# A plain first cycle for the first expert of a Strassen-like stage, and an earlier place for the rounding of raw weight blocks

## The chip, the cores and the metric

The kernel runs on one core of a Trainium2 chip. The metric is the device time of one execution in microseconds (us). In the text and the rows, PE is TensorE, PEld its weight loads, ACT is ScalarE, DVE is VectorE, POOL is GpSimd and SP is SyncE.

## The reference

The reference is a chain: a dense mixture of eight experts and a shared one (the stage "cond", which the change touches), an attention with distances, a second dense-and-typed feed-forward, and a transformer block with routed experts. The stage in question computes, for x of 32 x 64 tokens by 256:

```python
g = jnp.einsum('bsd,edf->ebsf', h, Wg)
u = jnp.einsum('bsd,edf->ebsf', h, Wu)
expert_outs = jnp.einsum('ebsf,efd->ebsd', jax.nn.silu(g) * u, Wd)
expert_output = jnp.einsum('be,ebsd->bsd', gating_probs, expert_outs)
shared = jnp.einsum('bsf,fd->bsd', jax.nn.silu(h @ Sg) * (h @ Su), Sd)
return (1.0 - sg) * expert_output + sg * shared
```

with D = 256 and F = 1024, everything in float32.

## The kernel before, in words

The stage is `paired_experts` (from L222). It holds E = 9 experts (eight and the shared one). A product in float32 is made of three matmuls of rounded parts: high by high, high by low, low by high (`product`, L310). The high part is a rounding copy on ScalarE, the low part a subtraction on POOL (weights) or VectorE (x and the hidden values).

Per expert there are CY = 8 cycles: J = 4 blocks j of the hidden dimension (a pair of 128 rows each) by 2 halves p of the tokens (1024 tokens each, a left and a right side of 512). A cycle does two `quad`s, u = 0 for the gate matrix and u = 1 for the up matrix. Each quad is a 2 x 2 by 2 x 2 block product with seven products in Winograd's form (P1 to P7) instead of eight: it needs the sums S1 to S4 of weight blocks and T1 to T4 of x blocks, and additions of results on the way. The additions: `keep` on ScalarE copies P1 and P5 out of PSUM, `combine` (L544, L547) and `lower_right` (L554) on VectorE add. Between the products of a quad TensorE does the down projections of the cycle before (`down`, four groups of six matmuls in a cycle), so a full cycle is 42 + 24 = 66 matmuls of 512 columns.

Behind the products: ScalarE takes the silu of the four quarters of the gate result (L452), VectorE multiplies by the four of the up result (`hidden`, L561), ScalarE rounds (`round_hidden`), VectorE splits off the low part (`split`, L566), and TensorE uses both in the next cycle's `down`.

The weights of the next expert are prepared meanwhile. `raws(e, j)` rounds the three raw blocks that are used as they are (two ScalarE copies), and POOL splits them (L662, L663) and then makes the four sums in place in the loaded buffer (L665 to L670). `sums(e, j)` rounds the sums (one ScalarE copy) and the block of the down matrix, POOL splits both (L680, L686). The order is written out by hand in `tasks`, which both engines call at the end of their part of cycle c: c = 5, 6, 7 do `raws` 0, 1, 2 of the next expert, c = 6, 7 also `sums` 0, 1 ahead of it; c = 0 does `sums` 2 and `raws` 3 of the own expert, c = 1 `sums` 3. SyncE loads the next expert's weights when the last split of the own ones is done.

The first expert is different. x comes as four tiles of 512 tokens. TensorE turns (transposes) tiles 0 and 1 into the four y_ps banks, ScalarE and VectorE copy them out (`keep_raw`), and from these copies T1 to T4 are made (VectorE), rounded (ScalarE, `round_x`) and split (VectorE, `split_x`). Tiles 2 and 3 are turned between the products of cycle 0. POOL makes the second half's T values (`t_right`, L696 to L701) after a DMA has copied the first half of x to memory (`spilled[0]`, tensor x_saved), since they are written over it; the raw block 2 and its sums lie behind them in POOL's order. Ahead of that copy SyncE issues the loads of x, of the constants and of small tensors (L3138).

Of the kernel before, what the change touches and what calls it, by code (L numbers as in the profile page):

```python
# [6 lines left out]
F32 = mybir.dt.float32  # L7
# [195 lines left out]
def paired_experts(nc, m, x, saved, stage, experts, hyp):  # L203
# [20 lines left out]
    dn_rounded, dn_ready = sem("dn_rounded"), sem("dn_ready")  # L224
    p1_done, p2_done, p3_done, p4_done, p5_done, p6_done, p7_done = (sem(f"p{i}_done") for i in range(1, 8))
# [11 lines left out]
    with ExitStack() as s:  # L237
# [7 lines left out]
        h_hi, h_lo = sb("h_hi", [P, 4, TW], F32R), sb("h_lo", [P, 4, TW], F32R)  # L245
# [8 lines left out]
        t_room = [h, flat[:, 0:4 * TW].rearrange("p (i n) -> p i n", i=4)]  # L254
# [24 lines left out]
        with nc.Block() as block:  # L279
# [29 lines left out]
            def _(pe):  # L309
                def product(bank, e, c, u, w, i, opens, done):  # L310

                    p, j = divmod(c, J)
                    for k, (ws, xs) in enumerate(((w_hi, x_hi(i, 1, cols(p))), (w_hi, x_lo[:, i:i + 1, cols(p)]), (w_lo, x_hi(i, 1, cols(p))))):
                        ins = pe.matmul(bank, ws[:, j, u, w], xs.rearrange("p o n -> p (o n)"), start=(opens and k == 0), stop=(k == 2), skip_group_check=True)  # L314
                    ins.then_inc(done, 1)
# [23 lines left out]
                def quad(e, c, u, between):  # L339
                    p, j = divmod(c, J)  # L340
                    q, g = 2 * (CY * e + c) + u, CY * e + c
                    start = isinstance(g, int) and g == 0
                    if p == 0 and u == 0:
                        pe.wait_ge(up_ready, J * e + j + 1)
                    if start and u == 0:
                        pe.wait_ge(x_lo_dve, 2)
                    if isinstance(g, int) and g == J and u == 0:
                        pe.wait_ge(x_lo_pool, 7)
                    if u == 1:
                        pe.wait_ge(silu_done, 4 * g + 1)  # L350
                    elif not start:
                        pe.wait_ge(h_made, 4 * (g - 1) + 1)
                    product(bank_a, e, c, u, A11, B11, True, p1_done)
                    if u == 1:
                        pe.wait_ge(silu_done, 4 * g + 2)
                    elif not start:
                        pe.wait_ge(h_made, 4 * (g - 1) + 2)
                    product(bank_d, e, c, u, S1, T1, True, p5_done)
                    if start and u == 0:
                        pe.wait_ge(x_lo_dve, 3)  # L360
                    if not start:
                        pe.wait_ge(h_made if u == 1 else silu_done, 4 * g)
                    product(bank_b[u], e, c, u, S2, T2, True, p6_done)
                    pe.wait_ge(p1_kept, q + 1)
                    product(bank_a, e, c, u, A12, B21, False, p2_done)
                    between(0)
                    if start and u == 0:
                        pe.wait_ge(x_lo_dve, 6)
                    pe.wait_ge(u4_made, q + 1)
                    product(bank_d, e, c, u, S4, B22, False, p3_done)  # L370
                    product(bank_b[u], e, c, u, S3, T3, False, p7_done)
# [4 lines left out]
                def turn_right(n):  # L376
                    if n == 0:
                        pe.wait_ge(raw_by_act, 2)
                        pe.wait_ge(raw_by_dve, 2)
                    pe.wait_ge(x_loaded[2 + n], 16)  # L380
                    for k in range(KC):
                        turn(2 + n, k)

                def expert(e, first, last):
                    for c in range(CY):
                        for u in range(UPS):
                            if first and c == 0:
                                quad(e, c, u, turn_right if u == 0 else lambda n: None)
                                continue
# [7 lines left out]
                for t in range(2):  # L397
                    pe.wait_ge(x_loaded[t], 16)
                    for k in range(KC):
                        turn(t, k)  # L400
# [6 lines left out]
            def _(act):  # L407
# [28 lines left out]
                def keep(e, c, u):  # L436
# [3 lines left out]
                    if not (isinstance(q, int) and q == 0):  # L440
                        act.wait_ge(u2_made, q)
                    copy(p1_row[:], bank_a).then_inc(p1_kept, 1)
                    act.wait_ge(p5_done, q + 1)
                    if u == 1:
                        act.wait_ge(silu_done, 4 * g + 3)
                    elif not (isinstance(g, int) and g == 0):
                        act.wait_ge(h_made, 4 * (g - 1) + 3)
# [22 lines left out]

                def expert(e, first, last):
                    for c in range(CY):
                        g = CY * e + c
                        keep(e, c, 0)
                        if not (first and c == 0):
                            pe_e, pe_c = (e, c - 1) if c > 0 else (e - 1, CY - 1)
                            round_hidden(pe_e, pe_c, 11, 3)
                            round_hidden(pe_e, pe_c, 21, 4)
                            act.wait_ge(h_ready, 4 * g)
                        silu(e, c, p2_done, bank_a, 0)  # L480
                        silu(e, c, p3_done, bank_d, 1)
                        silu(e, c, c22_made, p5_row[:], 2)
                        silu(e, c, p4_done, bank_b[0], 3)
                        keep(e, c, 1)
                        if first and c == 0:
                            act.wait_ge(turned, 2 * TT)
                            for t in range(2):
                                keep_raw(1, t)
# [16 lines left out]
                        tasks(e, c, first, last, sums, raws)  # L505
# [4 lines left out]

                stage.load_up_first(act, experts(0)[0:2])
# [3 lines left out]
                for t in range(2):  # L515
                    keep_raw(0, t)
                act.wait_ge(t_made, 1)
                round_x(0, T1, 1)
                act.wait_ge(raw_by_dve, 1)
                round_x(0, B11, 2)  # L520
                act.wait_ge(t_made, 2)
                round_x(0, T2, 1)
                act.wait_ge(w_summed, 4)
                copy(w_hi[:, 0, :, S2:S1 + 1].rearrange("p u (k s) n -> p u k (s n)", k=KC), raw_up[:, :, :, pair(0)]).then_inc(sums_rounded, 1)
                round_x(0, B22, 1)
                act.wait_ge(t_made, 4)
                round_x(0, T3, 1)
                round_x(0, T4, 1)
                raws(0, 1)
# [5 lines left out]
            def _(dve):  # L535
# [3 lines left out]
                def combine(e, c, u):  # L539

                    q = 2 * (CY * e + c) + u
                    dve.wait_ge(p1_kept, q + 1)
                    dve.wait_ge(p6_done, q + 1)
                    dve.tensor_tensor(bank_b[u], p1_row[:], bank_b[u], ALU.add).then_inc(u2_made, 1)  # L544
                    dve.wait_ge(p5_kept, q + 1)
                    dve.wait_ge(u2_made, q + 1)
                    dve.tensor_tensor(bank_d, p5_row[:], bank_b[u], ALU.add).then_inc(u4_made, 1)  # L547

                def lower_right(e, c, u):
# [3 lines left out]
                    dve.wait_ge(u4_made, q + 1)  # L553
# [43 lines left out]
                def split_x(i, n, count):  # L597
                    dve.wait_ge(x_rounded, count)
                    src = raw[0][:, 0:2, sides[0]] if i == B11 else raw[0][:, 1:2, sides[1]] if i == B22 else t_room[0][:, i - T1:i - T1 + n]
                    dve.tensor_tensor(x_lo[:, i:i + n, cols(0)], src, x_hi(i, n, cols(0)), ALU.subtract).then_inc(x_lo_dve, 1)  # L600

                def expert(e, first, last):
                    for c in range(CY):
                        p, j = divmod(c, J)
                        combine(e, c, 0)
                        if not (first and c == 0):
                            pe_e, pe_c = (e, c - 1) if c > 0 else (e - 1, CY - 1)
# [2642 lines left out]
```

## Time and profile before

| | |
|---|---|
| median of 3 runs | 2121.78 us (2121.76 to 2122.68) |
| the profiled execution's own time | 2122.61 us |
| its span | 2120.8 us |
| busy shares: PE, DVE, ACT, POOL | 91%, 70%, 53%, 42% |
| mean granted TensorE clock | 0.959 |

A busy time is the sum of the instructions of an engine. A row of the timeline has its start from the span's start, its duration, the engine, line, operation, tiles written and read, and in brackets the idle time before it and what ended it. The expert stage lasts from the start to about 1105 us; the part around the first expert to about 110 us.

### The profile page before, as it was taken

The page shows a single profiled execution, that of the slowest core. Times are in us where ns is not written, and L with a number is a line of the kernel's source. Part 1 is how long each engine was busy: PE and PEld are TensorE (multiplying, and loading weights), DVE is VectorE, ACT ScalarE, POOL GpSimd, SP SyncE. Part 2 cuts the span into 40 slices and gives each one's busy share as a digit, 9 for nine tenths or more (in the row PEclk, how much of TensorE's full clock was granted, in tenths as well). Part 3 has the DMA queues.
Part 4 walks back from the last instruction along what each step waited for, and adds up shares of the span by engine and source line. Part 5 has one row for each costly group of instructions (what it writes and reads, how often), then busy time and mean ns, then how long its engine had stood idle before and what let it go on. Part 6 is the DMA issues. An engine that isn't in the chain of part 4 may idle for free. (4 is left out here: it accounts for less than half of the span.)

```text
span 2120.8 us, 35303 instructions
## 1 busy us (share of the span) xinstructions
PE 1928.9 (91%) x12206; PEld 1612.7 (76%) x12206; DVE 1476.1 (70%) x2400; ACT 1115.2 (53%) x2117; POOL 897.8 (42%) x858
## 2 busy tenths in 40 slices
PE   5999999999999999999998677999899766959998
PEld 4778878787887878788787466788799645849998
DVE  6777777767777776777876896433588575856776
ACT  4555554545555464555554697232355364636664
POOL 5442241504224150422400185220388234968885
PEclk9999999999999999999999788999999887979999
DMA  4101010010101001010102201310256114556661
GB/s 151 60 1 60 1 59 0 0 59 0 59 0 59 0 0 59 0 59 0 28 1 60 61 3 41 120 45 5 70 195 200 53 29 131 184 183 208 210 214 54
DMA packets 96322, 144.51 MB, mean 68 GB/s; under 512 B 15358, under 2 KB 72608, under 8 KB 96096
## 3 DMA queue, kind: packets, MB, share of 16 engines
q1 hardware_dynamic: 89168, 127.21, 18.6%
q0 software_dynamic: 4928, 12.86, 1.7%
q10 hardware_dynamic: 2128, 3.15, 0.4%
q8 instruction: 60, 0.98, 0.2%
q14 instruction: 38, 0.31, 0.0%
HBM read 111.46 MB, written 14.16 MB: 59 GB/s over the span
## 5 line engine op out<-in xcount | busy, mean ns | idle before, releaser
L314 PE MATMUL ps<-cond_x_lo,cond_w_hi 128*128 128x512 f32 x1008 | 393.7, 391 | 0.0
L408 ACT ACTIVATE cond_h_hi<-cond_h 128x512 fp32r<-128x512 f32 x288 | 177.1, 629 | 266.5 <-DVE cond_h L561 266.4
L566 DVE TENSOR_TENSOR cond_h_lo<-cond_h,cond_h_hi 128x512 fp32r<-128x512 f32 x288 | 261.8, 938 | 4.1 <-ACT cond_h_hi L408 0.3
L314 PE MATMUL ps<-cond_x_hi_first,cond_w_hi 128*128 128x512 f32 x576 | 229.5, 398 | 17.7 <-DVE ps L547 8.8
L662 POOL TENSOR_TENSOR cond_w_lo<-cond_stage_up,cond_w_hi 128x512 fp32r<-128x512 f32 x36 | 57.5, 1596 | 439.0 <-ACT cond_w_hi L408 439.0
L330 PE MATMUL ps<-cond_h_hi,cond_d_hi 128*128 128x512 f32 x576 | 227.4, 395 | 7.3 <-DVE cond_h_lo L566 7.1
L314 PE MATMUL ps<-cond_x_hi_first,cond_w_lo 128*128 128x512 f32 x576 | 225.1, 391 | 0.0
L330 PE MATMUL ps<-cond_h_hi,cond_d_lo 128*128 128x512 f32 x576 | 224.7, 390 | 0.0
L330 PE MATMUL ps<-cond_h_lo,cond_d_hi 128*128 128x512 f32 x576 | 224.3, 389 | 0.0
L452 ACT ACTIVATE cond_h<-ps 128x512 f32<-128x512 f32 x216 | 121.5, 597 | 193.3 <-DVE cond_h_lo L566 151.9
L544 DVE TENSOR_TENSOR ps<-cond_p_row,ps 128x512 f32<-128x512 f32 x144 | 99.8, 693 | 175.7 <-PE ps L314 175.7
L314 PEld LDWEIGHTS ps<-cond_x_lo,cond_w_hi 128*128 128x128 f32 x1008 | 189.9, 188 | 38.0
L408 ACT ACTIVATE cond_p_row<-ps 128x512 f32<-128x512 f32 x288 | 172.1, 598 | 46.5 <-PE ps L314 34.1
L680 POOL TENSOR_TENSOR cond_w_lo<-cond_stage_up,cond_w_hi 128x1024 fp32r<-128x1024 f32 x36 | 86.8, 2410 | 224.9 <-ACT cond_w_hi L408 224.9
L561 DVE TENSOR_TENSOR cond_h<-cond_h,ps 128x512 f32<-128x512 f32 x216 | 147.4, 683 | 45.9 <-PE ps L314 45.9
L314 PE MATMUL ps<-cond_x_hi,cond_w_hi 128*128 128x512 f32 x432 | 169.0, 391 | 1.0 <-DVE cond_p_row L554 1.0
L314 PE MATMUL ps<-cond_x_hi,cond_w_lo 128*128 128x512 f32 x432 | 168.5, 390 | 0.0
L314 PEld LDWEIGHTS ps<-cond_x_hi_first,cond_w_hi 128*128 128x128 f32 x576 | 108.3, 188 | 55.5 <-DVE ps L547 24.4
L330 PEld LDWEIGHTS ps<-cond_h_hi,cond_d_hi 128*128 128x128 f32 x576 | 108.1, 188 | 40.3 <-issue 9.4
L314 PEld LDWEIGHTS ps<-cond_x_hi_first,cond_w_lo 128*128 128x128 f32 x576 | 108.6, 188 | 22.9
L330 PEld LDWEIGHTS ps<-cond_h_hi,cond_d_lo 128*128 128x128 f32 x576 | 108.1, 188 | 23.0
L1031 DVE SCALAR_TENSOR_TENSOR dense_h_lo<-ps,dense_h_hi 128x512 fp32r<-128x512 f32 x64 | 44.3, 692 | 116.4 <-ACT dense_h_hi L977 116.3
(408 smaller groups left out, 5190.2 us busy)
## 6 DMA issues: line engine op xcount, KB each, us to landing
moe_stage_up<-in_L_ffn_expert_wv SPq DMA_DIRECT2D x22, 1024.0 KB, 9.3
typed_stage_up<-in_L_cond_wi SPq DMA_DIRECT2D x11, 1024.0 KB, 4.9
typed_stage_dn<-in_L_cond_wo SPq DMA_DIRECT2D x11, 1024.0 KB, 5.6
moe_stage_dn<-in_L_ffn_expert_proj SPq DMA_DIRECT2D x11, 1024.0 KB, 5.6
cond_stage_up<-in_L_cond_Wg SPq DMA_DIRECT2D x7, 1024.0 KB, 5.1
cond_stage_up<-in_L_cond_Wu SPq DMA_DIRECT2D x7, 1024.0 KB, 7.2
cond_stage_dn<-in_L_cond_Wd SPq DMA_DIRECT2D x7, 1024.0 KB, 9.5
rope_v_now<-rope_v_blk SPq DMA_DIRECT2D x16, 272.0 KB, 2.4
```

The lines of the kernel that those rows point to most:

```text
L314: ins = pe.matmul(bank, ws[:, j, u, w], xs.rearrange("p o n -> p (o n)"), start=(opens and k == 0), stop=(k == 2), skip_group_check=True)
L330: ins = pe.matmul(y_ps[side][d], w[:, 2 * j + r, d * P:(d + 1) * P], xs[:, tile], start=(j == 0 and r == 0 and k == 0), stop=(j == J - 1 a ...
L408: copy = lambda dst, src: act.activation(dst, src, ACT.Copy)
L452: act.activation(h[:, tile], src, ACT.Silu).then_inc(silu_done, 1)
L544: dve.tensor_tensor(bank_b[u], p1_row[:], bank_b[u], ALU.add).then_inc(u2_made, 1)
L561: dve.tensor_tensor(h[:, tile], h[:, tile], src, ALU.mult).then_inc(h_made, 1)
L566: dve.tensor_tensor(h_lo[:, tile], h[:, tile], h_hi[:, tile], ALU.subtract).then_inc(h_ready, 1)
L662: pool.tensor_tensor(w_lo[:, j, :, A11:A12 + 1], raw_up[:, :, :, upper(j)], w_hi[:, j, :, A11:A12 + 1], ALU.subtract)
L680: pool.tensor_tensor(w_lo[:, j, :, S2:S1 + 1].rearrange("p u (k s) n -> p u k (s n)", k=KC), raw_up[:, :, :, pair(j)], w_hi[:, j, :, S2:S1 ...
L1031: dve.scalar_tensor_tensor(h_lo[:, st % HB], up_ps[st % 2][0], 0.0, h_hi[:, st % HB], ALU.max, ALU.subtract).then_inc(h_ready, 1)
```

## The change

Two things are changed.

Cycle 0 of the first expert no longer uses the seven products. `plain` multiplies the blocks as they are: eight products for each matrix, accumulated in pairs in PSUM, so that no `keep` and no `combine` is needed; VectorE copies one of the four results out of PSUM (`plain_copy`) so that the following steps find it where it was. One more block (the lower left one) is needed raw; it lies in the room of S1 of block 3. x is rounded straight from PSUM (`raw_block`) and split straight from PSUM (`split_block`), with the fourth x block in the room of T4 of the other half; the copies `keep_raw` come later. T1 to T4 are made and split during cycle 0, for cycle 1, in a tile of their own. The transposes of tiles 1 to 3 stand between the plain products. `raws(0, 1)` on ScalarE now stands between the roundings of the first and the second x tile, and on POOL ahead of the split of sums 0. Since cycle 0 keeps nothing, the counts of five semaphores start lower by two.

In all other cycles, of all experts, `tasks` is split in two: `raw_tasks` stands behind the first silu of the cycle on ScalarE and ahead of the sums on POOL, `sum_tasks` stays at the end.

```diff
-        def tasks(e, c, first, last, sums, raws):
-            nxt = e + 1
+        def raw_tasks(e, c, first, last, raws):
             if c == 0 and not first:
-                sums(e, 2)
                 raws(e, 3)
-            elif c == 1 and not first:
-                sums(e, 3)
             elif c >= 5 and not last:
-                if c > 5:
-                    sums(nxt, c - 6)
-                raws(nxt, c - 5)
+                raws(e + 1, c - 5)
+        def sum_tasks(e, c, first, last, sums):
+            if c < 2 and not first:
+                sums(e, c + 2)
+            elif c > 5 and not last:
+                sums(e + 1, c - 6)
...
 # TensorE
+                def plain():
+                    for u in range(UPS):
+                        plain_left(u)
+                        turn_tile(1 if u == 0 else 3)
+                        plain_lower_left(u)
+                        plain_right(u)
+                        if u == 0:
+                            turn_tile(2)
+                        plain_lower_right(u)
+                def plain_left(u):
+                    if u == 0:
+                        pe.wait_ge(plain_ready, 1)
+                        pe.wait_ge(x_lo_dve, 1)
+                    else:
+                        pe.wait_ge(silu_done, 1)
+                    multiply(bank_a, 0, u, A11, B11, cols(0), True).then_inc(p1_done, 1)
+                    if u == 0:
+                        pe.wait_ge(x_lo_dve, 2)
+                    multiply(bank_a, 0, u, A12, B21, cols(0), False).then_inc(p2_done, 1)
...
 # ScalarE
+                def plain():
+                    silu(0, 0, p2_done, bank_a, 0)
+                    act.wait_ge(t_made, 1)
+                    round_x(0, T1, 1)
+                    silu(0, 0, p3_done, bank_d, 1)
+                    act.wait_ge(t_made, 2)
+                    round_x(0, T2, 1)
+                    silu(0, 0, c22_made, p5_row[:], 2)
+                    silu(0, 0, p4_done, bank_b[0], 3)
+                    act.wait_ge(t_made, 4)
+                    round_x(0, T3, 1)
+                    round_x(0, T4, 1)
+                    act.wait_ge(turned, 2 * TT)
+                    for t in range(2):
+                        keep_raw(1, t)
...
+                def first_group(e, c, first, last):
+                    g = CY * e + c
+                    keep(e, c, 0)
...
+                    act.wait_ge(h_ready, 4 * g)
+                    silu(e, c, p2_done, bank_a, 0)
+                    raw_tasks(e, c, first, last, raws)
+                    silu(e, c, p3_done, bank_d, 1)
+                    silu(e, c, c22_made, p5_row[:], 2)
+                    silu(e, c, p4_done, bank_b[0], 3)
...
                 raws(0, 0)
-                act.wait_ge(turned, 2 * KC)
...
+                copy(w_hi[:, J - 1, :, S1], raw_up[:, :, 0, lower(0)]).then_inc(plain_rounded, 1)
+                for k in range(KC):
+                    act.wait_ge(turned, k + 1)
+                    raw_block(k, 0)
+                raws(0, 1)
+                for k in range(KC):
+                    act.wait_ge(turned, KC + k + 1)
+                    raw_block(k, 1)
...
 # POOL
-                raws(0, 0)
+                pool.wait_ge(w_rounded, 1)
+                split_upper(0).then_inc(plain_ready, 1)
+                split_lower(0).then_inc(plain_ready, 1)
+                pool.wait_ge(plain_rounded, 1)
+                pool.tensor_tensor(w_lo[:, J - 1, :, S1], raw_up[:, :, 0, lower(0)], w_hi[:, J - 1, :, S1], ALU.subtract).then_inc(plain_ready, 1)
+                pool.wait_ge(plain_ready, 3)
+                sum_blocks(0, 0)
+                raws(0, 1)
                 split_sums(0, 0)
-                raws(0, 1)
                 split_sums(0, 1)
```

## Rows read from the trace of the kernel before

**Rows 1.** The page, busy time, share of the span, instructions.

```profile
PE 1928.9 (91%) x12206; PEld 1612.7 (76%) x12206; DVE 1476.1 (70%) x2400; ACT 1115.2 (53%) x2117; POOL 897.8 (42%) x858
```

**Rows 2.** Timeline of TensorE, first products and starts of cycles 2, 4, 5.

```profile
21.80 0.79 PE L314 MATMUL ps<-cond_x_hi_first,cond_w_hi 128*128 128x512 f32 x1 [7.86 <-POOL cond_w_lo L680]
22.39 0.63 PE L314 MATMUL ps<-cond_x_lo,cond_w_hi 128*128 128x512 f32 x1
22.82 0.63 PE L314 MATMUL ps<-cond_x_hi_first,cond_w_lo 128*128 128x512 f32 x1
...
56.78 0.50 PE L314 MATMUL ps<-cond_x_hi_first,cond_w_hi 128*128 128x512 f32 x1
...
92.38 0.39 PE L314 MATMUL ps<-cond_x_hi_first,cond_w_hi 128*128 128x512 f32 x1
...
107.40 0.39 PE L314 MATMUL ps<-cond_x_hi_first,cond_w_hi 128*128 128x512 f32 x1
```

**Rows 3.** Timeline of SyncE's queue: the copy of x, two experts' loads.

```profile
21.48 13.37 SPq L291 DMA_DIRECT2D x_saved<-sum  x2
...
306.26 0.37 SPq L191 DMA_DIRECT2D cond_stage_up<-in_L_cond_Wg  x1
...
797.53 0.37 SPq L191 DMA_DIRECT2D cond_stage_up<-in_L_cond_Wg  x1
```

**Rows 4.** Timeline, 0 to 22 us, POOL and VectorE.

```profile
8.14 1.26 POOL L662 TENSOR_TENSOR cond_w_lo<-cond_stage_up,cond_w_hi 128x512 fp32r<-128x512 f32 x1 [7.33 <-ACT cond_w_hi L408]
...
12.32 0.72 POOL L670 TENSOR_TENSOR cond_stage_up<-cond_stage_up 128x256 f32<-128x256 f32 x1
...
19.23 2.52 POOL L680 TENSOR_TENSOR cond_w_lo<-cond_stage_up,cond_w_hi 128x1024 fp32r<-128x1024 f32 x1 [6.18 <-ACT cond_w_hi L408]
19.46 2.83 DVE L644 TENSOR_TENSOR cond_h<-sum 128x512 f32<-128x512 f32 x1
```

**Rows 5.** DMA issues, 0 to 10 us: count, KB, us to landing.

```profile
cond_stage_up<-in_L_cond_Wu ACTq DMA_DIRECT2D x1, 768.0 KB, 10.8
```

**Rows 6.** DMA, 20 to 34 us: packets, then issues.

```profile
DMA packets 1536, 0.07 MB, mean 5 GB/s; under 512 B 1521, under 2 KB 1521, under 8 KB 1536
...
x_saved<-sum SPq DMA_DIRECT2D x1, 1024.0 KB, 17.8
```

**Rows 7.** Timeline of POOL, 41 to 57 us.

```profile
41.54 1.74 POOL L696 TENSOR_TENSOR sum<-sum 128x512 f32<-128x512 f32 x1
43.24 1.28 POOL L697 TENSOR_TENSOR sum<-sum 128x512 f32<-128x512 f32 x1
...
54.33 2.41 POOL L680 TENSOR_TENSOR cond_w_lo<-cond_stage_up,cond_w_hi 128x1024 fp32r<-128x1024 f32 x1 [1.17 <-ACT cond_w_hi L408]
```

**Rows 8.** Timeline of ScalarE, 485 to 497 us (fourth expert).

```profile
485.27 0.93 ACT L408 ACTIVATE cond_w_hi<-cond_stage_up 128x512 fp32r<-128x512 f32 x2
...
495.91 1.09 ACT L452 ACTIVATE cond_h<-ps 128x512 f32<-128x512 f32 x2 [1.97 <-DVE cond_h_lo L566]
```

**Rows 9.** Timelines of POOL (two rows) and VectorE, 501 to 511 us.

```profile
501.55 2.40 POOL L680 TENSOR_TENSOR cond_w_lo<-cond_stage_up,cond_w_hi 128x1024 fp32r<-128x1024 f32 x1 [9.42 <-ACT cond_w_hi L408]
...
505.16 1.75 POOL L662 TENSOR_TENSOR cond_w_lo<-cond_stage_up,cond_w_hi 128x512 fp32r<-128x512 f32 x1
...
504.83 0.92 DVE L561 TENSOR_TENSOR cond_h<-cond_h,cond_p_row 128x512 f32<-128x512 f32 x1 [0.19 <-DVE cond_p_row L554]
505.68 2.92 DVE L566 TENSOR_TENSOR cond_h_lo<-cond_h,cond_h_hi 128x512 fp32r<-128x512 f32 x2
...
509.90 0.70 DVE L547 TENSOR_TENSOR ps<-cond_p_row,ps 128x512 f32<-128x512 f32 x1
```

**Rows 10.** Timeline of TensorE, 490 to 511 us.

```profile
490.64 0.39 PE L314 MATMUL ps<-cond_x_hi_first,cond_w_hi 128*128 128x512 f32 x1
...
505.78 0.39 PE L314 MATMUL ps<-cond_x_hi_first,cond_w_hi 128*128 128x512 f32 x1
...
510.65 0.50 PE L314 MATMUL ps<-cond_x_hi_first,cond_w_hi 128*128 128x512 f32 x1 [0.34 <-DVE ps L547]
```

More of the change, by code:

```diff
@@ L341, in quad @@
                     q, g = 2 * (CY * e + c) + u, CY * e + c
-                    start = isinstance(g, int) and g == 0
+                    early = isinstance(g, int) and g == 1 and u == 0
                     if p == 0 and u == 0:
                         pe.wait_ge(up_ready, J * e + j + 1)
-                    if start and u == 0:
-                        pe.wait_ge(x_lo_dve, 2)
                     if isinstance(g, int) and g == J and u == 0:
@@ L350, in quad @@
                         pe.wait_ge(silu_done, 4 * g + 1)
-                    elif not start:
+                    else:
                         pe.wait_ge(h_made, 4 * (g - 1) + 1)
@@ L396, in _ @@
                 pe.wait_ge(ident_loaded, 16)
[L397 to L400, printed above, removed]
+                turn_tile(0)
                 run(pe, expert)
@@ L439, in keep @@
                     act.wait_ge(p1_done, q + 1)
-                    if not (isinstance(q, int) and q == 0):
-                        act.wait_ge(u2_made, q)
+                    if not (isinstance(q, int) and q == 2):
+                        act.wait_ge(u2_made, q - 2)
                     copy(p1_row[:], bank_a).then_inc(p1_kept, 1)
@@ L445, in keep @@
                         act.wait_ge(silu_done, 4 * g + 3)
-                    elif not (isinstance(g, int) and g == 0):
+                    else:
                         act.wait_ge(h_made, 4 * (g - 1) + 3)
@@ L473, in expert @@
                         g = CY * e + c
[L474 to L484, printed above, removed]
                         if first and c == 0:
-                            act.wait_ge(turned, 2 * TT)
-                            for t in range(2):
-                                keep_raw(1, t)
+                            plain()
+                        else:
+                            first_group(e, c, first, last)
+                            keep(e, c, 1)
                         if first and c < J:
@@ L504, in expert @@
                                 round_x(1, T4, 1)
-                        tasks(e, c, first, last, sums, raws)
+                        sum_tasks(e, c, first, last, sums)
                         if last and c == 4:
@@ L609, in expert @@
                             split(pe_e, pe_c, 21, 4)
-                        lower_right(e, c, 0)
-                        if first and c == 0:
+                            lower_right(e, c, 0)
+                        else:
+                            plain_copy(0)
+                            for i in (T1, T2, T3, T4):
+                                split_t(i)
+                            dve.wait_ge(x_lo_dve, 8)
                             dve.wait_ge(turned, 2 * TT)
@@ L621, in expert @@
                             take(of_e, of_p, RIGHT if j == 0 else LEFT, first)
-                        combine(e, c, 1)
+                        if not (first and c == 0):
+                            combine(e, c, 1)
                         hidden(e, c, p2_done, bank_a, 0)
                         hidden(e, c, p3_done, bank_d, 1)
-                        lower_right(e, c, 1)
+                        if first and c == 0:
+                            plain_copy(1)
+                        else:
+                            lower_right(e, c, 1)
                         dve.wait_ge(c22_made, 2 * (CY * e + c) + 2)
@@ L630, in expert @@
                         hidden(e, c, p4_done, bank_b[1], 3)
[L632 to L634 removed]
+                for t in range(2):
+                    for k in range(KC):
+                        split_block(k, t)
+                    dve.wait_ge(turned, KC * (t + 1))
+                    keep_raw(0, t)
                 dve.wait_ge(raw_by_act, 2)
                 dve.wait_ge(raw_by_dve, 2)
[L637 removed]
+                low, tm = raw[0], t_first
                 dve.tensor_tensor(tm[:, 0], low[:, 0, sides[1]], low[:, 0, sides[0]], ALU.subtract).then_inc(t_made, 1)
@@ L733, in expert @@
                     for c in range(CY):
-                        tasks(e, c, first, last, sums, raws)
+                        raw_tasks(e, c, first, last, raws)
+                        sum_tasks(e, c, first, last, sums)
                 run(pool, expert)
```

151 lines of the change are left out of this document (91 added, 60 removed).

## Prediction

> **What bounds the kernel now.** I read the page first: TensorE is busy 91% of the span, so a change pays only where it starts TensorE earlier or takes away one of its pauses [rows 1]. Then I read TensorE's timeline at the starts of the first expert's cycles [rows 2]: the first product begins at 21.80 us, cycle 2 at 56.78, cycle 4 at 92.38 and cycle 5 at 107.40. From 92.38 to 107.40 is 15.02 us; a whole cycle is 66 matmuls, so one is 0.2275 us and this cycle has no pause. [...] Last, the loads of one expert's weights are issued once per expert at the same place of it: from 306.26 to 797.53 us is four experts, 122.82 us each [rows 3]. Eight clean cycles are 120.16 us, so each expert loses 2.66 us. Where it is lost I saw in a repeated pattern: in the three cycles that follow a cycle in which ScalarE both rounds sums and rounds raw blocks (cycles 7, 0 and 1), 0.88 us each. Such blocks lie behind cycles 6 and 7 of experts 0 to 7 and behind cycle 0 of experts 1 to 8: 24 places, 21.1 us.
>
> **The start, step by step.** Removed: the wait of the first product for the split sums of block 0 (POOL's L680, 19.23 to 21.75 us) [rows 4]. Added: TensorE does 48 products' matmuls in cycle 0 instead of 42 (eight blocks of three, times two matrices): 6 x 0.2275 = 1.4 us. The first plain product needs the split of the raw block (8.14 + 1.26 = 9.40 us on POOL [rows 4]), one round and one split of x from PSUM behind the first transposes, and so begins near 10 us instead of 21.80. [...] Working the orders forward, cycle 0 ends near 26.5 us; cycle 1 needs the sums of block 1, which ScalarE rounds behind the four silus and the x copies at about 26, and POOL splits in 2.4 us: cycle 1 begins near 29 us.
>
> That lead of some 9 us does not last. Before cycle 2 POOL must do, in order, the differences of the second half of x (L696 to L701), raw block 2 and the split of its sums. The first of these waits for the copy of x to memory, x_saved. It is issued at 21.48 us, held by SyncE's own slow issues ahead of it and not by its data, and lands 17.8 us later, at 39.3; in the 14 us after its issue the queue moves only 0.07 MB, in 1521 packets under 512 B [rows 3, 6]. None of those issues is changed. So POOL, done with the earlier work near 31 us, stands until 39.3. Before, it came there at 41.54, and the split of sums 2 ended at 54.33 + 2.41 = 56.74, TensorE starting cycle 2 at 56.78: a POOL-bound start [rows 2, 7]. The chain is 15.2 us with 1.2 us of waiting for ScalarE and with slowed operations: 1.28 us is the best of the four differences, the others take up to 1.74 [rows 7]. Alone: 4 x 1.28 + 4.90 (the six operations of a raw block, 8.14 to 13.04 [rows 4]) + 1.2 + 2.41 = 13.6; TensorE and VectorE are less in the way, so I take 14.3, half way. Cycle 2 begins at 39.3 + 14.3 = 53.6, 3.2 us earlier; 2.2 us if the chain takes the full 15.2, 3.9 at 13.6. [...] Cycle 2 is a little less crowded. I take **3.5 us** for the start, bounds 1.5 and 5.5.
>
> **The moved rounding of raw blocks.** It is no part of the start: it holds for every expert. ScalarE's two copies (0.93 us [rows 8]) move from the end of a cycle to behind its first silu, and with them POOL's six operations. On ScalarE: in the cycle that begins at 490.64 the first silu runs from 495.91 for 0.55 us, the copies to 497.4, the second silu to 498.0, the third to 498.5. TensorE wants the second silu for the second product of u=1, due 490.64 + 36 x 0.2275 = 498.83; the fourth silu waits for a product that is done about 498.5. So the 0.93 us lie in a hole of 0.9 to 1.1 us and cost nothing; without that cover they cost 0.93 us in 32 cycles.
>
> On POOL: now the sums split starts at 501.55, the down split follows, and from 505.16 the raw block (1.75 us for an operation that takes 1.26 alone) [rows 4, 9]. VectorE in that time works on operands that lie only in SBUF: 504.83 (0.92), then the pair from 505.68 (2.92 us where two of 0.70, overlapping by a tenth, would take 1.3). The down projection due at 505.78 + 12 x 0.2275 = 508.51 can't start before the pair ends, at 508.60; the addition L547 ends at 510.60, and the product due 18 matmuls behind 505.78, at 509.88, starts at 510.65 [rows 9, 10]. After: POOL's raw block starts at 497.45 and takes 4.9 to 5.0 us, to 502.4, while VectorE stands idle or has an operand in PSUM; L547, which has one, takes 0.70 with POOL busy. The sums split, ready at 501.5, runs 502.45 to 504.85, the down split (503.95 to 505.16 now: 1.25) to 506.1, and then POOL is quiet. VectorE has three such operations to do from 504.83.
>
> How they meet decides the sum. VectorE's L644 at 19.46 takes 2.83 us and ends 0.54 us after POOL's L680 does, at 21.75 [rows 4]: it stood until the whole POOL operation was through, so the engines take turns. Then VectorE's three follow the down split or share turns with it: 506.1 + 1.9 = 508.0 instead of 508.60. L547 ends the same 2.0 us later, 510.0, and the product starts 0.17 late, plus 0.11 for a restart (0.50 against 0.39 us for the matmul after a pause [rows 10]): 0.28 stays, 0.60 of 0.88 is won. 24 x 0.60 = **14.4 us**, bounds 10 and 21.1. Read as a common loss of pace instead (1.87 us lost in 3.44 us of overlap, 0.54 per us), VectorE would lose 0.8 us, end at 507.5, and nothing would stay: 24 x 0.88 = 21.1. [...]
>
> **Sum.** Against the profiled execution's own time, 2122.6 us (span 2120.8; the median of the runs is 2121.8, 0.8 lower): 3.5 + 14.4 = 17.9, so 2104.7; the median should lie up to 0.8 below it, and I say 2104.
>
> **Rivals.** (a) Loss of pace, not turns: 2122.6 - 3.5 - 21.1 = 2098. For it speak the many middle durations, against it L644. (b) x_saved lands early and doesn't hold POOL: POOL goes on at 31, cycle 2 starts near 49, the start gives 7.5: 2122.6 - 7.5 - 14.4 = 2100.7. The 1521 small packets speak against it. (c) The pauses move instead of going: the sums split, now behind the raw block, or the accumulations of the down projection in cycle 0 collide with POOL so that 0.8 of the 0.88 stay: 2122.6 - 3.5 - 24 x 0.08, about 2117 to 2119. The margin is thin: 508.0 against 508.60. (d) Slower: the copies behind the first silu make the second silu late for TensorE. It decides once that silu comes more than 0.9 us later than worked out above; at 0.8 us of stall and restart in each of 32 cycles, 25.6 us, with the gain of 3.5 and 14.4: 2122.6 + 7.7 = 2130. For it: the silu waits for the splits of VectorE (to 495.9), late by any slip; against it: the slip delays TensorE as well.
>
> **From these to the numbers.** Chances: forecast 0.55, (a) 0.15, (b) 0.07, (c) 0.14, (d) 0.09. The forecast's own range is 2122.6 - 5.5 - 17 to 2122.6 - 1.5 - 10, 2100 to 2111. The range given, 2096 to 2113, adds (a) and (b) and leaves out (c), (d) and the odd tail: about 0.2 to 0.25. 0.2% is 4.2 us, about what a measurement of this kernel can tell from no change. Faster by more: forecast, (a), (b) and a little of (c), 0.80; within it: most of (c), 0.11; slower 0.09.
>
> **What would show it.** Right: the first product near 10 us, cycle 1 near 29, POOL's L696 counterpart waiting for the landing of x_saved, TensorE idle some 6 us before a cycle 2 that starts at 53 to 54.5; loads of the experts 121.0 us apart (120.2 under (a), 122.5 under (c)); VectorE's pair of splits ending 0.6 us sooner, no wait of the down projection, a wait of 0.1 to 0.2 us for L547's counterpart. Wrong: idle time of TensorE ended by a silu (d), a pair of splits as long as now (c), a POOL that never waits for x_saved (b). Wrong also if the order of small loads or the clock of later stages moved the rest of the span, where I expect an equal shift.

## The result and the profile after

The changed kernel takes 2100.8 us in the median of 4 runs (2099.61 to 2101.13), the kernel before 2122.2: the ratio is 0.9898, with a 95% interval of 0.9881 to 0.9915. That is 21.4 us less. The forecast was 2104, range 2096 to 2113, 17.9 us less. The profiled execution took 2100.97 us, its span is 2099.1.

The page of the changed kernel: busy time, share of the span and instructions; the row answers to [rows 1]. TensorE's share is the same, though the span is shorter, and VectorE lost 44 us of busy time and POOL 45. The additions that cycle 0 no longer makes are a small part of it; most is waiting: an instruction of VectorE or POOL that stands until one of the other engine is through counts as busy while it stands. The splits of hidden values and the multiplications without an operand in PSUM, 360 in all, take 0.68 to 2.87 us each, and what they take over 0.70 us is 82 us before and 38 after. On POOL the first operation of a raw block takes 1.27 to 1.76 us, 57 us in sum before (L662) and 47 after (L752).

```profile
PE 1917.7 (91%) x12212; PEld 1613.0 (77%) x12212; DVE 1431.7 (68%) x2398; ACT 1104.0 (53%) x2116; POOL 852.4 (41%) x859
```

Those waits can be seen in one group by line (busy us, mean ns), first of the kernel before, then of the one after: the split of hidden values, 288 times, falls from 938 to 719 ns. That is 61 us less; the multiplications give some of it back, since they stand longer now (below).

```profile
L566 DVE TENSOR_TENSOR cond_h_lo<-cond_h,cond_h_hi 128x512 fp32r<-128x512 f32 x288 | 261.8, 938 | 4.1 <-ACT cond_h_hi L408 0.3
```

```profile
L640 DVE TENSOR_TENSOR cond_h_lo<-cond_h,cond_h_hi 128x512 fp32r<-128x512 f32 x288 | 201.0, 719 | 15.9 <-ACT cond_h_hi L460 9.2
```

**The start.** Timeline of TensorE after, at the first product and the starts of cycles 1, 2, 4 and 5; it answers to [rows 2].

```profile
9.93 0.77 PE L317 MATMUL ps<-cond_x_hi_first,cond_w_hi 128*128 128x512 f32 x1 [0.65 <-DVE cond_x_lo L677]
...
28.90 0.47 PE L317 MATMUL ps<-cond_x_hi_first,cond_w_hi 128*128 128x512 f32 x1 [2.65 <-POOL cond_w_lo L783]
...
54.43 0.79 PE L317 MATMUL ps<-cond_x_hi_first,cond_w_hi 128*128 128x512 f32 x1 [8.45 <-POOL cond_w_lo L783]
...
89.51 0.39 PE L317 MATMUL ps<-cond_x_hi_first,cond_w_hi 128*128 128x512 f32 x1
...
104.53 0.39 PE L317 MATMUL ps<-cond_x_hi_first,cond_w_hi 128*128 128x512 f32 x1
```

The first product begins at 9.93 us. Cycle 1, at 28.90, is 9.5 us earlier than before (38.44). Then TensorE stands for 8.45 us, and cycle 2 is only 2.35 us earlier; at cycle 4 the lead is 92.38 - 89.51 = 2.87 us. What POOL waited for stands in its own timeline, which answers to [rows 7]: the first difference of the right half waits 8.74 us for the copy x_saved, as the prediction had it, and the split of sums 2 ends at 54.38.

```profile
40.31 1.29 POOL L799 TENSOR_TENSOR sum<-sum 128x512 f32<-128x512 f32 x1 [8.74 <-DMA x_saved<-sum]
...
52.02 2.36 POOL L783 TENSOR_TENSOR cond_w_lo<-cond_stage_up,cond_w_hi 128x1024 fp32r<-128x1024 f32 x1 [1.17 <-ACT cond_w_hi L460]
```

**The experts.** SyncE's queue after; it answers to [rows 3]. From 298.98 to 781.28 us is four experts, 120.58 us each instead of 122.82: 2.24 us per expert.

```profile
21.37 6.17 SPq L295 DMA_DIRECT2D x_saved<-sum  x2
...
298.98 0.37 SPq L191 DMA_DIRECT2D cond_stage_up<-in_L_cond_Wg  x1
...
781.28 0.37 SPq L191 DMA_DIRECT2D cond_stage_up<-in_L_cond_Wg  x1
```

The books: 2.87 us at cycle 4; 21.01 at the first load of the next stage (hyp_wo, issued at 1044.17 before and 1023.16 after), so 18.1 lie in the experts; 0.6 more in all that follows, which I can't place and which a measurement can't tell from nothing.

In one of the 24 places the timelines of POOL, VectorE, ScalarE and TensorE after read as follows; they answer to [rows 8 to 10].

```profile
487.50 1.29 POOL L752 TENSOR_TENSOR cond_w_lo<-cond_stage_up,cond_w_hi 128x512 fp32r<-128x512 f32 x1 [9.95 <-ACT cond_w_hi L460]
...
492.47 2.41 POOL L783 TENSOR_TENSOR cond_w_lo<-cond_stage_up,cond_w_hi 128x1024 fp32r<-128x1024 f32 x1
494.83 1.29 POOL L789 TENSOR_TENSOR cond_d_lo<-cond_stage_dn,cond_d_hi 128x512 fp32r<-128x512 f32 x1
...
495.04 1.63 DVE L635 TENSOR_TENSOR cond_h<-cond_h,cond_p_row 128x512 f32<-128x512 f32 x1 [0.19 <-DVE cond_p_row L628]
496.59 1.47 DVE L640 TENSOR_TENSOR cond_h_lo<-cond_h,cond_h_hi 128x512 fp32r<-128x512 f32 x2
...
486.49 0.93 ACT L460 ACTIVATE cond_w_hi<-cond_stage_up 128x512 fp32r<-128x512 f32 x2
487.32 0.59 ACT L504 ACTIVATE cond_h<-ps 128x512 f32<-128x512 f32 x1
...
495.99 0.39 PE L317 MATMUL ps<-cond_x_hi_first,cond_w_hi 128*128 128x512 f32 x1
...
500.12 0.50 PE L317 MATMUL ps<-cond_x_hi_first,cond_w_hi 128*128 128x512 f32 x1
```

POOL's raw block now stands ahead of the sums, from 487.50. VectorE's multiplication, issued at 495.04, takes 1.63 us: it stands until POOL's down split is through at 496.12, and ends 0.55 us behind that. POOL is idle during the pair of splits behind it: 1.47 us instead of 2.92. From the issue of the multiplication to the end of the pair is 3.02 us, before 3.77 [rows 9]. The product due at 495.99 + 18 x 0.2275 = 500.09 starts at 500.12.

This place, behind cycle 6, is the best of the three kinds. The lengths of TensorE's cycles show all of them. They are means over experts 2 to 7, in us, from the starts of each cycle's first product in the timelines (the kernels of experiments 4, 5 and 8 are described below):

| | cycle 0 | 1 | 2 to 4 | 5 | 6 | 7 | expert |
|---|---|---|---|---|---|---|---|
| before | 15.94 | 15.92 | 14.98 | 14.97 | 15.14 | 15.91 | 122.82 |
| after | 15.31 | 15.30 | 14.96 | 14.96 | 14.96 | 15.16 | 120.57 |
| experiment 4 | 15.00 | 14.96 | 14.96 | 14.98 | 14.99 | 14.99 | 119.79 |
| experiment 5 | 17.50 | 17.24 | 14.96 | 15.21 | 15.21 | 17.50 | 127.55 |
| experiment 8 | 15.85 | 14.96 | 14.96 | 15.85 | 15.85 | 15.84 | 123.22 |

The three late cycles (0, 1 and 7) give back 0.63, 0.63 and 0.74 us, 16.0 in the 24 places. Cycle 6, which follows a cycle with a raw block alone, gives 0.18, another 1.5 in eight experts; small differences in the others make the rest of the 18.1. What stays lost against a clean cycle of 14.96 is 0.35, 0.34 and 0.20 us.

### The profile page after: what moved, and what is told of

Read it like the earlier page. It is cut to its first block and busy times, and to the rows that moved or that the text cites. A ratio compares the mean times of both kernels' runs of the same rounds, so it can differ in the third digit from the quotient of the medians.

```text
span 2099.1 us, 35300 instructions
## 1 busy us (share of the span) xinstructions
PE 1917.7 (91%) x12212; PEld 1613.0 (77%) x12212; DVE 1431.7 (68%) x2398; ACT 1104.0 (53%) x2116; POOL 852.4 (41%) x859
## 3 DMA queue, kind: packets, MB, share of 16 engines
q1 hardware_dynamic: 89168, 127.21, 18.9%
## 5 line engine op out<-in xcount | busy, mean ns | idle before, releaser
L752 POOL TENSOR_TENSOR cond_w_lo<-cond_stage_up,cond_w_hi 128x512 fp32r<-128x512 f32 x36 | 46.9, 1303 | 588.2 <-ACT cond_w_hi L460 588.2
L640 DVE TENSOR_TENSOR cond_h_lo<-cond_h,cond_h_hi 128x512 fp32r<-128x512 f32 x288 | 201.0, 719 | 15.9 <-ACT cond_h_hi L460 9.2
L460 ACT ACTIVATE cond_p_row<-ps 128x512 f32<-128x512 f32 x284 | 167.1, 597 | 41.4 <-PE ps L317 33.6
L628 DVE TENSOR_TENSOR cond_p_row<-cond_p_row,ps 128x512 f32<-128x512 f32 x142 | 97.1, 684 | 45.1 <-PE ps L317 45.1
L373 PEld LDWEIGHTS ps<-cond_h_lo,cond_d_hi 128*128 128x128 f32 x576 | 108.3, 188 | 22.6
```

The costliest lines, as they stand in the source:

```text
L373: ins = pe.matmul(y_ps[side][d], w[:, 2 * j + r, d * P:(d + 1) * P], xs[:, tile], start=(j == 0 and r == 0 and k == 0), stop=(j == J - 1 a ...
L460: copy = lambda dst, src: act.activation(dst, src, ACT.Copy)
L628: dve.tensor_tensor(p5_row[:], p5_row[:], bank_b[u], ALU.add).then_inc(c22_made, 1)
L640: dve.tensor_tensor(h_lo[:, tile], h[:, tile], h_hi[:, tile], ALU.subtract).then_inc(h_ready, 1)
L752: return pool.tensor_tensor(w_lo[:, j, :, A11:A12 + 1], raw_up[:, :, :, upper(j)], w_hi[:, j, :, A11:A12 + 1], ALU.subtract)
```

## Experiments

All times are medians, beside runs of the kernel before on the same chip (2121.7 us in the first four, 2122.7 in the last four). "Places" are the 24 named in the prediction. In the cuts of code `...` stands for lines and arguments left out.

**1. Only the moved rounding, on the kernel before.** `tasks` is split in two as in the change, on POOL the raw tasks stand ahead of the sums, and nothing else is done.

```diff
                         silu(e, c, p2_done, bank_a, 0)
+                        raw_tasks(e, c, first, last, raws)
                         silu(e, c, p3_done, bank_d, 1)
...
-                        tasks(e, c, first, last, sums, raws)
+                        sum_tasks(e, c, first, last, sums)
```

> The kernel before with only the raw tasks moved behind the first silu of each cycle. My theory (VectorE and POOL take turns on operands that lie only in SBUF, and 24 places lose 0.88 us before and 0.14 after): 24 x 0.74 = 17.8 us, 2122.2 - 17.8 = 2104.4 us, within 1.5, with the experts' loads 120.6 us apart. Rival (most of the gain belongs to the start, and the later stages shift by other causes): above 2110 us. The two parts alone should sum to the whole within 1 us.

Measured: 2106.9 us, ratio 0.9925 (0.9909 to 0.9942). It is 1 us outside what I gave and below the rival's 2110. The gain, 14.8 us by the medians and 15.9 by the ratio (interval 12 to 19), is 70 to 75% of the whole. The experts are 120.74 us apart:

```profile
302.46 0.37 SPq L191 DMA_DIRECT2D cond_stage_up<-in_L_cond_Wg  x1
...
785.43 0.37 SPq L191 DMA_DIRECT2D cond_stage_up<-in_L_cond_Wg  x1
```

**2. Only the plain start.** The changed kernel with the raw tasks back at the end of the cycle, behind the sums, on ScalarE (shown) and on POOL.

```diff
-                    raw_tasks(e, c, first, last, raws)
...
                         sum_tasks(e, c, first, last, sums)
+                        raw_tasks(e, c, first, last, raws)
```

> The changed kernel with the raw tasks put back to the end of the cycle. Theory (the start is held by the landing of x_saved, near 40.3 us, so its lead of 9.5 us at cycle 1 shrinks to 2.9 at cycle 4): 2122.2 - 2.9 = 2119.3 us, within 0.8, loads of the experts 122.8 us apart. Rival (the start's gain also frees time in later cycles): below 2117 us.

Measured: 2119.2 us, ratio 0.9986 (0.9976 to 0.9995), as expected: the plain start is worth 2.5 to 3 us, and the experts are again 122.8 us apart (303.04 to 794.16 us for four). That is 12 to 14% of the whole gain. In the traces, up to the first load of the next stage, the two alone save 16.46 and 3.46 us, 19.9 together, and the whole change 21.01. I had expected the two alone to add up to the whole within 1 us: in the traces they lack 1.1, by the medians 17.3 us stand against 21.4, by the ratios 18.9. That was a miss, though the interval of experiment 1 alone is wider than the gap.

**3. The copy of x ahead of the small loads.** The changed kernel, with SyncE's small loads behind both copies and the gates in cycle 3, since they need these loads.

```diff
-                m.load_small(sp, small_loaded)
                 for p in range(PAIRS):
...
                     sp.dma_start(saved...).then_inc(spilled[p], 16)
+                m.load_small(sp, small_loaded)
...
-                        if first and c == 1:
+                        if first and c == 3:
                             gates()
```

> The changed kernel with the small loads issued behind both copies of x to memory, and the gates worked out in cycle 3 instead of 1. Theory: x_saved is issued near 16.7 us and lands near 21, POOL doesn't stop at its first difference of the right half, its chain of 14.3 us starts near 31.6, cycle 2 starts near 46 to 47 instead of 54.4; some contention with VectorE in cycle 1 gives back about 1 us: 2100.8 - 7 = 2093.8 us, within 1.5. Rival (POOL and VectorE collide so much in cycle 1 that the wait only changes its name): no more than 3 us faster, 2097.8 or above.

Measured: 2094.2 us, ratio 0.9868 (0.9852 to 0.9884). The copies are issued at 16.71, POOL goes on at 31.53 without a wait, and cycle 2 starts at 47.94 without one:

```profile
16.71 10.81 SPq L294 DMA_DIRECT2D x_saved<-sum  x2
...
31.53 1.73 POOL L799 TENSOR_TENSOR sum<-sum 128x512 f32<-128x512 f32 x1
...
47.94 0.39 PE L317 MATMUL ps<-cond_x_hi_first,cond_w_hi 128*128 128x512 f32 x1
```

So the landing of x_saved was what took back the start's lead: cycle 1 starts where it did (28.89), cycle 2 comes 6.5 us sooner, and the kernel gains 6.6. The gates moved too, and what that does alone was not run; the 6.5 us leave it little room. POOL's first difference takes 1.73 us here, with VectorE's splits under way, and 1.29 at 40.31 in the kernel after: its chain up to the split of sums 2 is 15.4 us long instead of 14.1, so some of the gain does go back in contention. It ends at 46.88, a microsecond ahead of cycle 2, and TensorE has no pause between 34 us and that start: it is TensorE itself that sets it now, with nine matmuls at a granted clock of 0.50 on the way (see the last section).

**4. The raw tasks one step earlier still**, ahead of ScalarE's wait for the splits and the first silu.

```diff
                     round_hidden(pe_e, pe_c, 21, 4)
+                    raw_tasks(e, c, first, last, raws)
                     act.wait_ge(h_ready, 4 * g)
                     silu(e, c, p2_done, bank_a, 0)
-                    raw_tasks(e, c, first, last, raws)
```

> The changed kernel with the raw tasks one step earlier still: ahead of the first silu, in the 1.8 us for which ScalarE waits there for VectorE's splits. Theory of turns: POOL's raw block ends 1.5 us sooner, the sums split then starts when ScalarE has rounded them, 0.7 us sooner, the down split ends at 0.3 instead of 1.1 us behind the issue of VectorE's multiplication, and the last 0.14 us of each of 24 places goes: 2100.8 - 3.4 = 2097.4 us, loads 120.2 us apart. Rival (common loss of pace, or what is left is a restart not due to POOL): no difference, 2100.8 within 0.8. Second rival (ScalarE reaches the copies before the last product of the previous cycle has left the weights' room and stands): slower than 2102.

Measured: 2094.9 us, ratio 0.9874 (0.9857 to 0.989): the direction of the theory of turns, and 2.5 us more than it gave. SyncE, POOL and VectorE in this kernel:

```profile
298.35 0.37 SPq L191 DMA_DIRECT2D cond_stage_up<-in_L_cond_Wg  x1
...
777.52 0.37 SPq L191 DMA_DIRECT2D cond_stage_up<-in_L_cond_Wg  x1
...
490.44 2.41 POOL L783 TENSOR_TENSOR cond_w_lo<-cond_stage_up,cond_w_hi 128x1024 fp32r<-128x1024 f32 x1 [1.12 <-ACT cond_w_hi L460]
492.81 1.30 POOL L789 TENSOR_TENSOR cond_d_lo<-cond_stage_dn,cond_d_hi 128x512 fp32r<-128x512 f32 x1
...
493.70 0.95 DVE L635 TENSOR_TENSOR cond_h<-cond_h,cond_p_row 128x512 f32<-128x512 f32 x1 [0.19 <-DVE cond_p_row L628]
494.57 1.47 DVE L640 TENSOR_TENSOR cond_h_lo<-cond_h,cond_h_hi 128x512 fp32r<-128x512 f32 x2
```

POOL now waits 1.12 us for ScalarE's sums, the down split ends 0.41 us behind the issue of the multiplication instead of 1.08, and TensorE has no pause left. The experts are 119.79 us apart: 528 matmuls without a pause take 119.8 us, 0.2269 each, not the 120.2 that I had from a single cycle. That is the miss. The 0.14 us per place that I expected to win was read at the best of the places; the table above has 0.35, 0.34 and 0.20 left in cycles 0, 1 and 7, and nearly all of it goes, 0.78 us per expert, 6.2 in eight. The kernel gained 5.9.

**5. The raw tasks 2.7 us later**, behind the fourth silu: the dose in the other direction.

```diff
                     silu(e, c, p2_done, bank_a, 0)
-                    raw_tasks(e, c, first, last, raws)
...
                     silu(e, c, p4_done, bank_b[0], 3)
+                    raw_tasks(e, c, first, last, raws)
```

> The changed kernel with the raw tasks behind the fourth silu instead of the first, some 2.7 us later. Theory of turns: POOL's raw block ends 2.6 us later, its sums split (2.41 us, one instruction) then runs when VectorE issues its multiplication on SBUF operands and keeps it waiting whole, the down split gets its turn before the second split of VectorE's; the pair of splits ends about 2.6 us too late, 2.7 us lost in each of 24 places against 0.14: 2100.8 + 61 = 2162 us, within 15. Theory of a common loss of pace (0.54 us per us of overlap): the pair ends about 1.1 us too late: 2100.8 + 26 = 2127 us, within 6. Rival (the place on ScalarE is what counts, and the hole there is as good behind the fourth silu): 2100.8 within 3.

Measured: 2157.1 us, ratio 1.0166 (1.0149 to 1.0182), within the range of the turns (2147 to 2177) and far above that of a common loss of pace (2121 to 2133). The rows show the turns one by one, POOL first:

```profile
517.26 2.40 POOL L783 TENSOR_TENSOR cond_w_lo<-cond_stage_up,cond_w_hi 128x1024 fp32r<-128x1024 f32 x1
519.61 1.74 POOL L789 TENSOR_TENSOR cond_d_lo<-cond_stage_dn,cond_d_hi 128x512 fp32r<-128x512 f32 x1
...
517.37 2.84 DVE L635 TENSOR_TENSOR cond_h<-cond_h,cond_p_row 128x512 f32<-128x512 f32 x1 [0.19 <-DVE cond_p_row L628]
520.13 2.37 DVE L640 TENSOR_TENSOR cond_h_lo<-cond_h,cond_h_hi 128x512 fp32r<-128x512 f32 x2
```

POOL's sums split starts 0.11 us ahead of VectorE's multiplication and holds it until 519.66, then it takes 0.55; POOL's down split, issued at 519.61, stands until 520.2 and takes 1.15 behind it; the first split of VectorE's, issued at 520.13, stands until 521.35. At the common pace of the other theory (0.54 us lost per us of overlap) the multiplication would have taken 0.69 / 0.46 = 1.5 us, and it took 2.84.

**6. Experiments 3 and 4 together.**

> The changed kernel with both edits that made it faster: the small loads behind the copies of x (6.6 us) and the raw tasks ahead of the first silu (5.9 us). They touch different stretches (cycles 1 and 2 of the first expert; cycles 7, 0 and 1 of each), so the gains should add: 2100.8 - 12.5 = 2088.3 us, within 1.5. Rival (with the start's wait gone, POOL's raw work of the first expert collides again and part comes back): 2091 or above.

Measured: 2087.3 us, ratio 0.9833 (0.9817 to 0.9849); the gains add. It is faster than the kernel before by 35 us and than the changed one by 13.

**7 and 8. Spare copies on ScalarE**, one and three, behind the raw copies of the changed kernel (n in the code is 1 or 3), to find how wide ScalarE's hole is.

```diff
                     raw_tasks(e, c, first, last, raws)
+                    if (c == 0 and not first) or (c >= 5 and not last):
+                        k = n * (4 * e + (0, 1, 2, 3)[max(0, c - 4)] - 1)
+                        for i in range(n):
+                            if not (isinstance(k, int) and k + i == 0):
+                                act.wait_ge(spare_done, k + i)
+                            copy(spare[:], x_hi(B11, 1, cols(0))...).then_inc(spare_done, 1)
                     silu(e, c, p3_done, bank_d, 1)
```

> The changed kernel with one more ScalarE copy of 128x512 elements, of no use, behind the raw copies in each of the 32 cycles that have them. If ScalarE's work there lies in a hole, as predicted (the second silu now ends 1.2 us before TensorE wants it), 0.6 us more costs nothing: 2100.8 within 1.5. If ScalarE's order is tight, 32 x 0.6 = 19 us more, 2120.

> The same with three such copies, each waiting for the one before it, about 1.9 us. The second silu then ends 0.65 us later than TensorE wants it, with a restart 0.76 us in 32 cycles, 24 us; the sums come 0.5 us or more too late for POOL in 24 of them and cost 0.6 us each, 14 us: 2100.8 + 38 = 2139 us, within 10. If the hole were wider than I think, no cost: 2101; if there were none, 32 x 1.9 = 61 us.

Measured: 2101.4 us with one, no cost; 2122.8 us with three, 22.0 us more. One copy fits, as expected. Of three I expected 38, and a little over half of that came. ScalarE and TensorE with three:

```profile
496.01 1.95 ACT L461 ACTIVATE cond_spare<-cond_x_hi_first 128x512 f32<-128x512 f32 x3
497.86 0.58 ACT L505 ACTIVATE cond_h<-ps 128x512 f32<-128x512 f32 x1
...
498.49 0.50 PE L318 MATMUL ps<-cond_x_hi_first,cond_w_hi 128*128 128x512 f32 x1 [0.45 <-ACT cond_h L505]
```

The second silu holds TensorE's second product of u=1: it comes 0.84 us behind the matmul before it instead of 0.23, 0.61 us and the restart behind it. In the table the four cycles with copies (5, 6, 7 and 0) take 15.85 us, 0.89 more than a clean one: 28 us in 32 cycles. Against that the 0.35, 0.34 and 0.20 us that the changed kernel still loses per expert are gone (cycle 1 is clean, and cycles 7 and 0 are no longer than 5 and 6): 7 us back, 21 in sum, and the experts are 123.2 us apart instead of 120.6. So the second term that I had put down, sums too late for POOL at a cost of 14 us, wasn't there and its opposite was: with TensorE late, VectorE is late as well, and finds more of POOL's work done (its multiplication stands until 505.09 and takes 1.04 us at 504.60, where it took 1.63).

## Why the prediction came out as it did

**The mechanism was right.** Both parts do what was worked out; the experiments back the two steps on which the number hung. The traces put 18.1 of 21.4 us where the prediction did, in the experts and not at the start, and experiments 1 and 2, 14.8 and 2.5 us alone, have the same order. The start's first product near 10 us (9.93), cycle 1 near 29 (28.90), POOL's wait for x_saved and TensorE's stop before cycle 2 are in the trace, and experiment 3 shows that the copy's place in SyncE's queue is the cause.

**Turns, not pace.** The prediction chose between them by one instruction [rows 4]. The trace after and experiment 5 settle it: each lengthened multiplication shown here ends 0.54 or 0.55 us behind the end of a POOL instruction (496.12, 494.11 and 519.66 us). The trace before could have settled it too. The multiplication of [rows 9] ends at 504.83 + 0.92 = 505.75, again 0.55 us behind POOL's down split:

```profile
503.91 1.29 POOL L686 TENSOR_TENSOR cond_d_lo<-cond_stage_dn,cond_d_hi 128x512 fp32r<-128x512 f32 x1
```

It is so everywhere: of these multiplications and of the splits of hidden values 134 take over 0.8 us in the trace before and 43 in the one after, and every one ends 0.53 to 0.57 us behind the end of a POOL instruction. The middle durations that spoke for a loss of pace are instructions issued in the middle of one of POOL's: each of these 177 starts with POOL busy. Rival (a) falls; the number alone wouldn't have shown it, since its 2098 lies 2.8 us from the result and mine 3.2. The operations with an operand in PSUM don't stand: L655 of the kernel after, which adds an operand in PSUM to one in SBUF, takes 0.69 us at 519.79 with POOL busy from 519.38 to 520.11, and the 235 additions, subtractions and multiplications of this kind that start with POOL busy in the first 1045 us of that trace take 0.67 to 0.70 us:

```profile
519.79 0.69 DVE L655 TENSOR_TENSOR sum<-sum,ps 128x512 f32<-128x512 f32 x1
...
519.38 0.73 POOL L755 TENSOR_TENSOR cond_w_lo<-cond_stage_up,cond_w_hi 128x256 fp32r<-128x256 f32 x1
```

**What was mis-sized.** Two terms, of opposite sign.

The moved rounding gave 18.1 us, not 14.4: less than the bound of 21.1 that the prediction gave this term, but more than the 17 that its own range was added up from. The prediction had 24 places that lose 0.88 us before and 0.28 after. By the table the 0.28 was close in the mean (0.35, 0.34 and 0.20) and the loss before was too small: 0.98, 0.96 and 0.95 us over a clean cycle of 14.96, where I had measured against a single one of 15.02. That makes 0.67 us won per place and 16.0 in all, not 0.60 and 14.4. The other 2 us are a term that the prediction left out: above all the 0.18 us lost in cycle 6, behind a cycle that has only a raw block, 1.5 us in eight experts. It could be seen in [rows 10]: from 490.64 to 505.78 us is 15.14.

In the place shown, the best of them, the late product starts 0.03 us late plus 0.11 for the restart (0.50 us against 0.39 for that matmul): 0.14 left. There POOL's raw block starts earlier than I had it. I read the first silu's time from the cycle that begins at 490.64, which was itself a little late; in the kernel after the sums split starts 2.57 us ahead of the multiplication where I had 504.83 - 502.45 = 2.38, and the pair of splits ends 0.75 us earlier, not 0.60. In the next place it is as predicted: the multiplication is issued at 510.22, the down split ends 1.22 us behind that (I had 1.27), and the pair ends 3.16 us behind it (I had 3.17). Without any loss an expert takes 119.79 us, 3.0 less than before, where I had put the ceiling at 2.66. That ceiling is also why rival (a) looked like 21.1.

The start gave 2.9 us, not 3.5. x_saved landed at 40.3 us, not 39.3; the chain behind it took 54.38 - 40.31 = 14.1 where I took 14.3. TensorE's stop was 8.45 us and not 6: cycle 1 had fewer pauses than I gave it. The bounds of 1.5 and 5.5 us that the forecast's range is added up from were my estimate, with an allowance for slow matmuls in cycle 2 that no run shows: the lead was 2.35 us at the start of cycle 2 and 2.87 at cycle 4, so the matmuls that came 0.43 us apart behind the stop took none of it.

**The rivals.** (b), a copy that doesn't hold POOL, is what experiment 3 makes: it then gives 6.6 us more, where the rival had 4. (c) fell with the margin: 3.02 us against 3.77. (d) is real as a mechanism and was far away: the second silu ended at 487.91, TensorE wanted it at 495.99 - 15.02 + 36 x 0.2275 = 489.16; one spare copy more costs nothing, three cost 22 us. The prediction had 0.9 us to the point of decision, the trace has 1.25.

**What stays open.** Experiment 1 has its experts at 120.74 us where the whole change has 120.58, with pauses of the same size; the mean distance of matmuls without a pause is 0.2274 us in it and 0.2271 after. What makes that difference I can't say. In eight experts it is 1.3 us, as much as the two parts alone lack to the whole in the traces. Cycles 0 and 1 keep more loss than cycle 7, and the multiplications ahead of them stand longer (1.77 us at 510.22 and 1.81 at 525.50 against 1.63); no experiment tells why.

## What to carry to other kernels

When two engines slow each other, ask first whether they share a rate or take turns; many instructions of the trace can tell, by when they end and not by how long they take. With turns, what counts is which long instruction is under way when the engine on the critical path issues. Moving 5 us of the other engine's work by a few microseconds was worth 0.7% here (experiment 1) with no work removed. Try the place in both directions: one step earlier won 6 us more, three steps later cost 56. When one place stands for 24, look at one of each kind: the place shown here kept 0.20 us, its neighbours 0.35. And a faster first step earns nothing until the slowest thing queued for the second is found; here it was a copy that stood behind small loads. They could be issued behind it, with their use two cycles later, at no cost.

## What the runs showed of the hardware

TensorE came to a granted clock of 0.50 behind a pause of only 2.65 us, and not at once: it had worked again for 1.3 us. In the timeline after, the distance from one matmul to the next is 0.23 to 0.30 us for the five from 28.90 on, behind the pause, and 0.43 from 30.20 to 33.2, where the records show a granted clock of 0.50 (0.57 over the whole window from 30 to 34). In experiment 3 a pause of 2.70 us ends at 28.89 and the clock reads 1.00 from there to 34.0, so a pause of this length was not enough by itself. Windows of the kernel after (start and end, length, busy time and instructions of each engine, granted clock, DMA share, GB/s):

```profile
28.00:30.00 2.00, 1.10 (x5) 0.95 (x6) 1.91 (x3) 0.63 (x1) 2.00 (x3) 1.00 0.05 0
30.00:34.00 4.00, 4.00 (x12) 3.01 (x11) 3.92 (x5) 2.75 (x5) 1.57 (x1) 0.57 0.05 0
...
54.00:57.00 3.00, 2.57 (x6) 2.09 (x7) 1.69 (x2) 2.39 (x5) 3.00 (x3) 0.50 0.00 0
```

The matmuls from 30.20 to 33.2 us cost some eight times 0.2 us, about 1.6, that didn't count, since cycle 2 waited for POOL anyway. In experiment 3 such a stretch does count: from 34.5 to 37.7 us, behind pauses of 0.41 and 1.36 us and a stretch in which TensorE was busy for 1.14 us of 2.5, nine matmuls run at a granted clock of 0.50, and cycle 2 starts as soon as TensorE is through. Behind the stop of 8.45 us the matmuls came 0.43 us apart for 3 us, at a granted clock of 0.50. In the kernel before, behind 7.86 idle ones, they came 0.43 us apart for 5 us, from 22.39 to 27.08, and there the clock in the records reads 1.00.

A copy stood long behind small packets in its queue: the copy of 1 MB, issued at 21.4 behind the small loads, landed at 40.3, and in the 14 us from 20 on the queue moved 0.01 MB in 1503 packets, all under 512 B. Issued ahead of the small loads (experiment 3), the two copies landed in 5.7 us (median).
